# A gated cross-attention and mixture-of-experts layer on one core: the routing arithmetic in fewer and smaller pieces, the last block's down products behind the first small tile, one gather sooner

## The chip, the cores and the metric

The kernel runs on one core of a Trainium2 chip. The metric is device time of one execution in microseconds (us), lower is better. The profile names the engines PE (TensorE, matrix products; PEld is its weight load), DVE (VectorE), ACT (ScalarE), POOL (GpSimd) and SP (SyncE, which only issues transfers here).

## The reference

The input is 4 x 1024 rows of 256 numbers. First each row attends, after a layer norm, to 77 context rows with 16 heads, and the output projection times tanh(g) is added to the row. Then comes the feed-forward part, which is all that the change touches:

```python
scores = softmax(xf @ gate_w.T)             # 4 experts
topk_w, topk_idx = top_k(scores, 2); topk_w /= topk_w.sum() + 1e-20
g = silu(xf @ eg[e].T); u = xf @ eu[e].T    # each expert, 256 -> 688
y = sum over e of comb[:, e] * ((g * u) @ ed[e].T)
y = y + (silu(xf @ sg.T) * (xf @ su.T)) @ sd.T   # the shared expert
x = x + tanh(g_ffn) * y
```

xf is the layer norm of the attended rows, 4096 of them, each sent to 2 of 4 experts, so there are 8192 row copies.

## The kernel before

**Stages.** The rows are worked in 16 units of 256. From 0 to about 308 us attention for all units runs, with the shared expert of units 0 to 6 woven in. From about 308 to 460 us ("late units" 7 to 15) the shared expert goes on, and between its pieces lie two other things: the transposes that bring the routed experts' matrices into place (`e_T(G)` on PE, then `e_hi(G)` on ACT and `e_lo(G)` on DVE, which split each into a high and a low part), and the routing arithmetic. From 460 to 773 us come 13 big blocks of 512 row copies that share one expert, from 773 us on 15 small tiles of 128 copies.

**Order.** Every engine has its own list of steps, written out by hand, and runs it in that order; a step waits on semaphores for what it needs. So a step that is late holds back all behind it on its engine. A unit n of the shared expert is, on PE, `gate_up(n, c)` for six chunks c = 0 to 5 and `down(n)`; on ACT `gate(n, c)` and `h_hi(n, c)`; on DVE `inner(n, c)` (two instructions, lines 2040 and 2045), `last_lo(n)` (line 2049) and `result(n)` (line 2058); on POOL `xn_lo(n)` and `h_lo(n, c)`. The waits that matter below:

- `gate_up(n, 3)` waits for `inner(n, 0)`, `gate_up(n, 4)` for `inner(n, 1)`, `gate_up(n, 5)` for `result(n - 1)`, which frees its bank.
- `down(n)` waits for `last_lo(n)`, and that for `h_hi(n, 5)`, and that for `inner(n, 5)`.
- `e_T(G)` waits for `e_lo(G - 2)`, since two banks are used in turn.
- ACT's list has `gate(9, 3)` behind `e_hi(5)`, which needs `e_T(5)`.

**Routing on DVE.** Its parts are small instructions on 4 to 128 numbers per partition, each linked to the next by a semaphore (`link`): `ranks()` (running counts per expert), `weights()`, `counts()` (reads what `bases()` on PE left in p_t: how many copies each expert gets), `starts()` (where each expert's blocks and small tiles begin), `numbered()`, `position(0)`, `position(1)`, `tiles_and_rows()`; `experts_of_tiles()` says which expert a block or tile has. `places(g)` and `rows_at(g)` (lines 2425, 2429) then build, for g = 0 to 7, 0/1 matrices whose product `spread(g)` on PE (line 3076) makes the table `slot_id` of rows, for the gathers.

**From big blocks to small tiles.** A block j has chunks c = 0 to 5: `big_gate_up` (line 619), `big_inner` and `big_h_lo` on DVE, `big_down(j, c)` (line 636) for t = 0 to 3, each t being 128 rows; t = 0, 1 go to bank p_f[0] and t = 2, 3 to p_f[1]. Chunks 4 and 5 of the last block's down products (24 and 8 products) are done before the small tiles begin. `big_result` (line 582, four times) moves p_f to big_yout, and POOL adds big_yout to the output rows by indirect DMA (line 505, four of them). A small tile j is, on PE, `gate_up(j)` (line 339, 18 calls in the profile's records), `x_T(j + 1)` (line 324, transposes of the gathered rows), `down(j - 1)` (line 350, 354), `hidden_T(j)` (line 364). Its DVE steps are the product `hid` (lines 294, 297), `x_lo(j + 1)` (line 274), `result(j - 1)` (line 286), and the low parts (lines 306 to 310). POOL gathers rows by an indirect DMA (line 199) and adds by another (line 220). Gathers 0 and 1 are issued one block before the end, gather 2 only after the last block's four adds. `hidden_T` writes its transposes to the two banks p_f, so `hidden_T(0)` first waits until the last `big_result` has read them.

Of the kernel before, what the change touches and what calls it, by code (L numbers as in the profile page):

```python
# [8 lines left out]
ALU = mybir.AluOpType  # L9
# [3 lines left out]
P = 128  # L13
# [134 lines left out]
def small_tiles(nc, v, sem, place, banks, s_add):  # L148
# [55 lines left out]
    def on_gpsimd(pool):  # L204
        gather = gathers(pool)

        def add(j, k):
            if not (isinstance(j, int) and j == 0):
                pool.wait_ge(s_add, added + 16 * (j - 1))
            pool.tensor_copy(add_at[k][:, :], slot_id[:, bass.ds(j + AFTER, 1)]).then_inc(s_add_at, 1)  # L210
            pool.wait_ge(s_add_at, j + 1)
            if isinstance(j, int) and j >= SM - 2:
                pool.wait_ge(s_add, added + 16 * j)
                settle(pool)
                pool.wait_ge(s_yo, j + 1)
            else:
                pool.wait_ge(s_yo, j + 1)
                pool.wait_ge(s_add, added + 16 * j)
                settle(pool)
            pool.indirect_dma_start(out, bass.IndirectOffsetOnAxis(add_at[k][:, :], 0),  # L220
                                    yout[k][:, :], None, compute_op=ALU.add).then_inc(s_add, 16)

        gather(2, 0)
        for j in range(2):
            gather(j + 3, 1 - j)
            add(j, j)
        with pool.Fori(1, (SM - 3) // 2) as h:
# [50 lines left out]

    def on_vector(dve):
        x_lo = x_low(dve)  # L280
# [8 lines left out]
        def step(j, k):  # L289
# [8 lines left out]
                                    p_gu[:, FF + CUT:2 * FF].unsqueeze(1).broadcast_to(twice),  # L298
                                    sil[:, CUT:FF].unsqueeze(1).broadcast_to(twice), ALU.mult).then_inc(s_dup, 1)
            if not last:  # L300
                x_lo(j + 1)
# [27 lines left out]
    def on_tensor(pe):  # L329
# [27 lines left out]

        def hidden_T(j):
            pe.wait_ge(s_hid, j + 1)
            wait(pe, s_hlo, j)  # L360
            for c in range(FC):
                if c == FC - 1:
                    pe.wait_ge(s_dup, j + 1)
                last = nc.tensor.transpose(p_h[c // 4][:, (c % 4) * P:(c % 4 + 1) * P], hid[:, c * P:(c + 1) * P],
                                           ident[:, :])
            last.then_inc(s_hT, 1)
# [39 lines left out]

        def run(gate_banks, hidden_banks):
            gate_banks()

            def step(j, k):  # L410
                fixed = isinstance(j, int)
                gate_up(j, expert(k))
                if not (fixed and j == SM - 1):
                    x_T(j + 1, 1 - k)
                if not (fixed and j == 0):
                    down(j - 1, expert(1 - k))
                if not (fixed and j == SM - 1):
                    hold(j + 1, 1 - k)
                if fixed and j == SM - 1:
                    last_hidden_T(j)  # L420
                else:
                    if fixed and j == 0:
                        hidden_banks()
                    hidden_T(j)
            hold(0, 0)
            tiles(pe, step)
            last_down(SM - 1, expert((SM - 1) % 2))
# [7 lines left out]
def big_tiles(nc, v, m, place, banks):  # L435
# [153 lines left out]
    def on_tensor(pe):  # L589
# [32 lines left out]

        def down(j, c):
            n = FC * j + c
# [7 lines left out]
            r = height(c) if c < FC - 1 else P  # L632
            for t in range(BT):
                at = slice(t * P, (t + 1) * P)
# [13 lines left out]
def attend_share_route(nc, v):  # L648
# [8 lines left out]
    with st:  # L657
# [37 lines left out]
        for k in range(2):  # L695
# [82 lines left out]
        w_parts = [sb(f"w_{s}", [P, NE], f32r) for s in ("hi", "lo")]  # L778
        tile_at, te, hit = (sb(n, [1, NX]) for n in ("tile_at", "te", "hit"))
        spare = sb("spare", [P, NS])  # L780
# [38 lines left out]
                                        "spare": rest.sb},  # L819
                           (p_s[:, 0:GUB, :].rearrange("p b n -> p (b n)"), p_m, p_f, p_t), s_add)  # L820
        big = big_tiles(nc, v, {"s_rows": s_rows, "s_xT": s_xnT, "s_xhi": s_xnhi, "s_xlo": s_xnlo, "s_whi": s_whi,
# [252 lines left out]
        def _(pool):  # L1074
# [360 lines left out]
            for j in range(NB):  # L1435
                if j + 2 < NB:
                    big_gather(j + 2)
                if j == NB - 2:
                    small_gather = late["gathers"](pool)
                    small_gather(0, 0)  # L1440
                    small_gather(1, 1)
                big_adds(j)
            late["gpsimd"](pool)
# [498 lines left out]
        def _(dve):  # L1942
# [411 lines left out]
            def counts():  # L2354
                dve.wait_ge(s_base, 1)
                link(nc.vector.tensor_copy(base[:, :], p_t[:, 0:E]))
                link(nc.vector.tensor_copy(count[:, :], p_t[:, E:2 * E]))
# [4 lines left out]
            def starts():  # L2362

                for e in range(1, E):
                    link(tt(blocks[:, e:e + 1], blocks[:, e - 1:e], blocks[:, e:e + 1], ALU.add))
                link(ts(big_end[:, :], blocks[:, :], float(NB), float(WIDE), ALU.min, ALU.mult))
                link(tt(rest_n[:, :], count[:, :], big_end[:, :], ALU.subtract))
                link(tt(rest_n[:, 1:E], rest_n[:, 1:E], big_end[:, 0:E - 1], ALU.add))
                link(ts(rest_n[:, :], rest_n[:, :], float(P - 1), None, ALU.add))
                link(nc.vector.tensor_copy(whole_i[:, :], rest_n[:, :]))  # L2370
# [4 lines left out]
                dve.wait_ge(s_zero, 10)  # L2375
                for e in range(1, E):
                    link(tt(small_at[:, e:e + 1], small_at[:, e - 1:e], rest_n[:, e - 1:e], ALU.add))
                link(nc.vector.scalar_tensor_tensor(out=jump[:, :], in0=small_at[:, :], scalar=float(AFTER * P),
                                                    in1=big_end[:, :], op0=ALU.add, op1=ALU.subtract))
                link(ts(base[:, :], base[:, :], -1.0, None, ALU.add))  # L2380
                link(tt(base[:, 1:E], base[:, 1:E], big_end[:, 0:E - 1], ALU.add))

            def numbered():
                wide_e = [P, E, NT]
                link(tt(cum[:, :, :], cum[:, :, :], base[:, :].unsqueeze(2).broadcast_to(wide_e), ALU.add))
                over = ttmp[:, :, :].rearrange("p t e -> p (t e)").rearrange("p (e t) -> p e t", e=E)
# [15 lines left out]
            def experts_of_tiles():  # L2402
                dve.wait_ge(s_iota, 7)
                link(nc.vector.tensor_copy(tile_at[:, :], tile_at_i[:, :]))
                for e in range(1, E):
                    into = te if e == 1 else hit
                    link(ts(into[:, 0:NB], tile_at[:, 0:NB], big_end[0:1, e - 1:e], None, ALU.is_ge))
                    link(ts(into[:, NB:NX], tile_at[:, NB:NX], small_at[0:1, e:e + 1], None, ALU.is_ge))
                    if e > 1:
                        link(tt(te[:, :], te[:, :], hit[:, :], ALU.add))  # L2410
                link(nc.vector.tensor_copy(expert_of[:, :], te[:, :]))
# [29 lines left out]
            def late_units():  # L2441
# [24 lines left out]
                e_lo(2)  # L2466
                inner(8, 3)
                inner(8, 4)
                e_lo(3)
                inner(8, 5)  # L2470
                e_lo(4)

                last_lo(8)
                weights()
                inner(9, 0)
                counts()
                starts()
                inner(9, 1)
                numbered()
                position(0)  # L2480
                position(1)
                tiles_and_rows()
                result(8)
                inner(9, 2)
                inner(9, 3)
                e_lo(5)
                inner(9, 4)
                inner(9, 5)
                e_lo(6)
# [20 lines left out]
                e_lo(11)  # L2510
                rows_at(2)
                inner(11, 0)
                e_lo(12)
# [42 lines left out]
                e_lo(21)  # L2556
                experts_of_tiles()
                places(7)
# [71 lines left out]
            for j in range(NB):  # L2630
                for c in range(FC):
                    big_step(j, c)
            for t in range(BT):
                big_result(NB - 1, t)
            late["vector"](dve)

        @block.tensor
        def _(pe):
# [442 lines left out]
            def late_units():  # L3081
# [154 lines left out]
            for j in range(NB):  # L3236
                for c in range(FC):
                    big_step(j, c)
            big_down(NB - 1, FC - 2)
            big_down(NB - 1, FC - 1)  # L3240
            late["tensor"](pe)(lambda: pe.wait_ge(s_hid, FC * (NU + NB)), lambda: pe.wait_ge(s_y, NU + 2 * NB))

# [24 lines left out]
```

## Time and profile before

| | us |
|---|---|
| median of 3 runs (890.25 to 891.5) | 890.29 |
| the profiled execution | 891.95 |
| its span, first to last instruction | 890.2 |
| PE busy | 851.2 (96% of the span) |
| DVE busy | 599.7 (67%) |
| ACT busy | 521.2 (59%) |
| POOL busy | 459.9 (52%) |

The mean granted TensorE clock is 0.986 of full speed (2.4 GHz). A row of the timeline gives start, duration, engine, line, operation and operands; in brackets is how long the engine sat idle before it and what ended that. "x3" is three instructions merged. PE's records are pipelined, so its pace is read from the distance of starts, not from durations.

### The profile page before, as it was taken

What the parts mean: (1) busy time and instruction counts of PE and PEld (TensorE: products, weight loads), DVE (VectorE), ACT (ScalarE), POOL (GpSimd) and SP (SyncE); (2) the same over time, 40 slices, a digit from 0 to 9 for tenths busy, and PEclk for the clock granted to TensorE, in tenths of its full rate; (3) what the DMA queues carried; (4) which work ended last, traced back from release to release, by engine and by line L of the source; (5) the groups of instructions that cost most, each with busy time, mean ns of one, the idle gap of its engine ahead of it and who ended that gap; (6) DMA issues with size and microseconds to landing.
All of it is one profiled execution on the core that took longest, in us unless ns stands there. A gap on an engine that the chain in (4) does not pass through costs nothing.

```text
span 890.2 us, 19216 instructions
## 1 busy us (share of the span) xinstructions
PE 851.2 (96%) x6271; PEld 745.9 (84%) x6272; DVE 599.7 (67%) x1259; ACT 521.2 (59%) x1846; POOL 459.9 (52%) x551
## 2 busy tenths in 40 slices
PE   8888999999999898999999999999999999989995
PEld 6566788878888798999988888888888888889994
DVE  6899899999998578878775555555555555434442
ACT  4989999999999343656464544444444544222221
POOL 5686767667665442676431454444444443444442
PEclk9799999999999999999999999999999999999998
DMA  7125223222312222423240333222222222232221
GB/s 217 41 79 175 68 89 93 89 66 91 101 62 85 71 73 68 135 84 119 82 142 24 49 48 48 46 39 41 38 42 42 43 46 36 31 45 45 35 37 22
DMA packets 56889, 62.06 MB, mean 70 GB/s; under 512 B 15643, under 2 KB 45184, under 8 KB 56800
## 3 DMA queue, kind: packets, MB, share of 16 engines
q1 hardware_dynamic: 42871, 43.15, 15.5%
q0 software_dynamic: 12864, 17.57, 12.5%
q8 instruction: 48, 0.79, 0.4%
q10 hardware_dynamic: 1064, 0.21, 0.1%
q14 instruction: 42, 0.34, 0.1%
HBM read 34.78 MB, written 25.82 MB: 68 GB/s over the span
## 4 chain that ended last, share of the span: by engine, by line
PE 82%; DVE 7%; ACT 4%; issue 3%; DMA 2%; POOL 1%; SPq 0%; DVEq 0%; POOLq 0%; ACTq 0%
PE p_s L619 22%; PE p_f L636 12%; PE p_f L2755 8%; PE p_s L339 6%; PE p_f L2800 4%; PE p_s L2755 4%; PE p_t L2686 3%; ACT prob L1478 3%; PE p_s L2672 3%; PE p_t L350 3%; PE p_m L2713 3%; PE p_m L2701 2%; PE p_m L2653 2%; PE p_s L2800 1%; PE p_s L2858 1%
## 5 line engine op out<-in xcount | busy, mean ns | idle before, releaser
L505 POOL DMA_INDIRECT out_rows<-big_yout,slot_id x52 | 86.5, 1664 | 156.4 <-DVE big_yout L582 144.6
L1478 ACT ACTIVATE prob<-p_s,negmax 128x77 f32<-128x77 f32 x512 | 161.2, 372 | 8.2 <-DVE negmax L2023 8.0
L533 ACT ACTIVATE big_sil<-p_s 128x512 f32<-128x512 f32 (+1 forms) x78 | 46.6, 597 | 143.3 <-PE p_s L619 143.3
L1478 ACT ACTIVATION_READ_ACCUMULATOR prob<-p_s,negmax 128x1 f32 x512 | 129.1, 255 | 0.0
L565 DVE TENSOR_TENSOR big_hid<-p_s,big_sil 128x512 f32<-128x512 f32 (+1 forms) x78 | 54.0, 692 | 99.5 <-ACT big_sil L533 99.5
L619 PE MATMUL p_s<-big_fxT_hi,big_w_hi 128*128 128x512 f32 (+1 forms) x286 | 113.9, 398 | 0.2 <-DVE big_w_lo L558 0.2
L619 PE MATMUL p_s<-big_fxT_lo,big_w_hi 128*128 128x512 f32 (+1 forms) x286 | 112.8, 394 | 0.0
L619 PE MATMUL p_s<-big_fxT_hi,big_w_lo 128*128 128x512 f32 (+1 forms) x286 | 112.2, 392 | 0.0
L1104 POOL TENSOR_TENSOR prob<-prob,rinv 128x616 f32<-128x616 f32 x64 | 78.5, 1236 | 62.3 <-DVE rinv L2030 62.3
L1123 POOL TENSOR_TENSOR shT_lo<-shid,shT_hi 128x256 fp32r<-128x256 f32 x80 | 63.2, 801 | 49.3 <-ACT shT_hi L1517 49.0
L636 PE MATMUL p_f<-wd_hi,big_hT_hi 128*128 (+1 forms) x312 | 85.6, 280 | 0.1
L636 PE MATMUL p_f<-wd_lo,big_hT_hi 128*128 (+1 forms) x312 | 85.3, 279 | 0.0
L2755 PE MATMUL p_f<-xnT_hi,swgu_hi 128*128 128x256 f32 x248 | 75.7, 305 | 2.0 <-DVE shid L2045 2.0
L636 PE MATMUL p_f<-wd_hi,big_hT_lo 128*128 x260 | 72.7, 280 | 0.0
L2755 PE MATMUL p_f<-xnT_hi,swgu_lo 128*128 128x256 f32 x248 | 69.7, 281 | 0.0
L2755 PE MATMUL p_f<-xnT_lo,swgu_hi 128*128 128x256 f32 x248 | 69.6, 281 | 0.0
L572 DVE TENSOR_TENSOR big_hT_lo<-big_hid,big_hT_hi 128x512 fp32r<-128x512 f32 (+1 forms) x65 | 44.9, 690 | 35.6 <-ACT big_hT_hi L538 35.6
L497 POOL DMA_INDIRECT big_xin<-xn_scratch,slot_id x52 | 51.3, 987 | 32.1 <-issue 17.2
L619 PEld LDWEIGHTS p_s<-big_fxT_hi,big_w_lo 128*128 128x128 f32 (+1 forms) x286 | 53.1, 186 | 13.0
L538 ACT ACTIVATE big_hT_hi<-big_hid 128x512 fp32r<-128x512 f32 (+1 forms) x78 | 49.3, 632 | 23.1 <-DVE big_hid L565 23.1
L636 PEld LDWEIGHTS p_f<-wd_hi,big_hT_hi 128*128 128x128 f32 (+1 forms) x312 | 58.7, 188 | 3.7 <-issue 0.3
L619 PEld LDWEIGHTS p_s<-big_fxT_hi,big_w_hi 128*128 128x128 f32 (+1 forms) x286 | 53.1, 186 | 10.2 <-issue 0.3
(336 smaller groups left out, 2561.3 us busy)
## 6 DMA issues: line engine op xcount, KB each, us to landing
xr<-in_x SPq DMA_DIRECT2D x16, 256.0 KB, 2.9
x_scratch<-xr SPq DMA_DIRECT2D x16, 256.0 KB, 2.5
xn_scratch<-xn SPq DMA_DIRECT2D x16, 256.0 KB, 2.1
xt_scratch<-xnT SPq DMA_DIRECT2D x16, 256.0 KB, 2.6
xin<-xt_scratch SPq DMA_DIRECT2D x16, 256.0 KB, 3.6
x1in<-x_scratch SPq DMA_DIRECT2D x16, 256.0 KB, 3.3
out_rows<-syout SPq DMA_DIRECT2D x16, 256.0 KB, 2.4
raw<-in_L_ffn_ed SPq DMA_DIRECT2D x4, 688.0 KB, 4.4
```

The lines of the kernel that those rows point to most:

```text
L339: last = nc.tensor.matmul(p_gu[:, g0:g1], fxT[a][:, c, :], wgu[b][:, bass.ds(e * KC + c, 1), g0:g1], start=(c == 0 and q == 0), stop=(c == ...
L497: pool.indirect_dma_start(xin[:, t, :], None, v["xn_d"], bass.IndirectOffsetOnAxis(slot_id[:, column(j, t)], 0)).then_inc(s_rows, 16)
L505: pool.indirect_dma_start(out, bass.IndirectOffsetOnAxis(slot_id[:, column(j, t)], 0), yout[:, t, :], None, compute_op=ALU.add).then_inc(s ...
L533: act.activation(sil[n % 2][0:r, :], p_gu[c % 2][0][0:r, :], ACT.Silu).then_inc(s_sil, 1)
L538: act.activation(hT[n % 3][0][0:r, :], hid[n % 2][0:r, :], ACT.Copy).then_inc(s_hhi, 1)
L565: nc.vector.tensor_tensor(hid[n % 2][0:r, :], up, sil[n % 2][0:r, :], ALU.mult).then_inc(s_hid, 1)
L619: last = nc.tensor.matmul(p_gu[c % 2][half][0:out_rows, :], lhsT, fxT[j % 2][x][:, k, :], start=(k == 0 and q == 0), stop=(k == KC - 1 and ...
L636: last = nc.tensor.matmul(p_y[t // 2][:, t % 2 * H:(t % 2 + 1) * H], hT[n % 3][h][0:r, at], wd[w][0:r, bass.ds(e * FC + c, 1), :], start=( ...
L1104: pool.tensor_tensor(pr_, pr_, rinv[:, t, m * HH:(m + 1) * HH].unsqueeze(2).broadcast_to([P, HH, SK]), ALU.mult).then_inc(s_P, 1)
L1123: pool.tensor_tensor(hT[1][:, c, :], hid[:, c, :], hT[0][:, c, :], ALU.subtract).then_inc(s_hlo, 1)
L1478: last = act.activation(prob[n % 2][t][:, m * PW + h * SK:m * PW + (h + 1) * SK], p_s[:, 2 * t + h // 4, col:col + SK], ACT.Exp, bias=negm ...
L2755: last = nc.tensor.matmul(bank[:, j * UT * P:(j + 1) * UT * P], swgu[w][:, k, j * SGU + c * P:j * SGU + (c + 1) * P], xns[x][:, n % 2, k, ...
```

## The change

The change has four parts.

1. *Routing on DVE, and `bases()` on PE.* In `counts()` the copy of `base` is taken out (it moves to the end of `starts()`); in `starts()` two chains of three additions become one scan each, a tensor_scalar is folded into its neighbour, and another into `numbered()`. In `experts_of_tiles()` compare and add become one instruction.
2. *Other places.* `bases()` moves from behind `gate_up(8, 5)` to behind `gate_up(8, 3)`. `weights()` goes from unit 9 to before `inner(8, 4)`, `counts()` to before `inner(8, 5)`, `starts()` before `inner(9, 0)`; `numbered()` and `result(8)` follow `inner(9, 1)`; `position(0)`, `position(1)` and `tiles_and_rows()` come behind `inner(9, 2)`, `inner(9, 3)` and `inner(9, 4)`. `experts_of_tiles()` goes from unit 14 to unit 11, before `inner(11, 0)`.
3. *Last block.* `big_down(12, 4)` is split: t = 0, 1 stay before `gate_up(0)` of the small tiles; t = 2, 3 and all of chunk 5 come behind it. The four `big_result(12, t)` move behind the product `hid` of small tile 0 on DVE. The small tiles' transposes use the banks p_s[3] and p_f[0], and only chunk 4 of `hidden_T(0)` waits, for the first two results.
4. *Gather 2* is issued before the last block's four adds on POOL, not after them.

```diff
@@ gathers and banks
-        gather(2, 0)
         for j in range(2):
             gather(j + 3, 1 - j)
             add(j, j)
...
+                if j == NB - 1:
+                    small_gather(2, 0)
                 big_adds(j)
...
-                           (p_s[:, 0:GUB, :].rearrange("p b n -> p (b n)"), p_m, p_f, p_t), s_add)
+                           (p_s[:, 0:GUB, :].rearrange("p b n -> p (b n)"), p_m, (p_s[:, 3, :], p_f[0]), p_t), s_add)
@@ small tiles, on DVE and PE
+            if isinstance(j, int) and j == 0:
+                last_results()
             if not last:
                 x_lo(j + 1)
...
             for c in range(FC):
+                if c == 4 and second_bank:
+                    second_bank()
...
                 gate_up(j, expert(k))
+                if fixed and j == 0:
+                    last_of_blocks()
@@ routing arithmetic
-                link(nc.vector.tensor_copy(base[:, :], p_t[:, 0:E]))
...
-                for e in range(1, E):
-                    link(tt(blocks[:, e:e + 1], blocks[:, e - 1:e], blocks[:, e:e + 1], ALU.add))
-                link(ts(big_end[:, :], blocks[:, :], float(NB), float(WIDE), ALU.min, ALU.mult))
-                link(tt(rest_n[:, :], count[:, :], big_end[:, :], ALU.subtract))
+                link(nc.vector.tensor_tensor_scan(big_end[:, :], fresh[0][:, 0:E], blocks[:, :], 0.0, ALU.mult, ALU.add))
+                link(ts(big_end[:, :], big_end[:, :], float(NB), float(WIDE), ALU.min, ALU.mult))
+                link(nc.vector.scalar_tensor_tensor(out=rest_n[:, :], in0=count[:, :], scalar=float(P - 1),
+                                                    in1=big_end[:, :], op0=ALU.add, op1=ALU.subtract))
                 link(tt(rest_n[:, 1:E], rest_n[:, 1:E], big_end[:, 0:E - 1], ALU.add))
-                link(ts(rest_n[:, :], rest_n[:, :], float(P - 1), None, ALU.add))
...
-                for e in range(1, E):
-                    link(tt(small_at[:, e:e + 1], small_at[:, e - 1:e], rest_n[:, e - 1:e], ALU.add))
+                link(nc.vector.tensor_tensor_scan(small_at[:, 1:E], fresh[0][:, 0:E - 1], rest_n[:, 0:E - 1], 0.0,
+                                                  ALU.mult, ALU.add))
...
-                link(ts(base[:, :], base[:, :], -1.0, None, ALU.add))
+                link(nc.vector.tensor_copy(base[:, :], p_t[:, 0:E]))
...
-                link(tt(cum[:, :, :], cum[:, :, :], base[:, :].unsqueeze(2).broadcast_to(wide_e), ALU.add))
+                link(nc.vector.scalar_tensor_tensor(out=cum[:, :, :], in0=cum[:, :, :], scalar=-1.0,
+                                                    in1=base[:, :].unsqueeze(2).broadcast_to(wide_e),
+                                                    op0=ALU.add, op1=ALU.add))
@@ experts_of_tiles
-                for e in range(1, E):
-                    into = te if e == 1 else hit
-                    link(ts(into[:, 0:NB], tile_at[:, 0:NB], big_end[0:1, e - 1:e], None, ALU.is_ge))
-                    link(ts(into[:, NB:NX], tile_at[:, NB:NX], small_at[0:1, e:e + 1], None, ALU.is_ge))
-                    if e > 1:
-                        link(tt(te[:, :], te[:, :], hit[:, :], ALU.add))
+                for a, b, ends in ((0, NB, big_end[0:1, 0:E - 1]), (NB, NX, small_at[0:1, 1:E])):
+                    link(ts(te[:, a:b], tile_at[:, a:b], ends[:, 0:1], None, ALU.is_ge))
+                    for e in range(1, E - 1):
+                        link(nc.vector.scalar_tensor_tensor(out=te[:, a:b], in0=tile_at[:, a:b], scalar=ends[:, e:e + 1],
+                                                            in1=te[:, a:b], op0=ALU.is_ge, op1=ALU.add))
@@ DVE's list, units 8, 9, 11 and 14
                 inner(8, 3)
+                weights()
                 inner(8, 4)
                 e_lo(3)
+                counts()
                 inner(8, 5)
                 e_lo(4)
 
                 last_lo(8)
-                weights()
+                starts()
                 inner(9, 0)
-                counts()
-                starts()
                 inner(9, 1)
                 numbered()
-                position(0)
-                position(1)
-                tiles_and_rows()
                 result(8)
                 inner(9, 2)
+                position(0)
                 inner(9, 3)
+                position(1)
                 e_lo(5)
                 inner(9, 4)
+                tiles_and_rows()
                 inner(9, 5)
...
                 rows_at(2)
+                experts_of_tiles()
                 inner(11, 0)
...
                 e_lo(21)
-                experts_of_tiles()
                 places(7)
@@ PE's list
                 gate_up(8, 3)
+                bases()
                 gate_up(8, 4)
                 e_T(3)
                 gate_up(8, 5)
-                bases()
                 e_T(4)
...
+            def last_of_blocks():
+                big_down(NB - 1, FC - 2, BT // 2, BT)
+                big_down(NB - 1, FC - 1)
...
+            big_down(NB - 1, FC - 2, 0, BT // 2)
+            late["tensor"](pe)(banks_of_gate, last_of_blocks, bank_of_hidden)
```

## Rows read from the trace of the kernel before

**Rows 1.** The page: the span.
```profile
span 890.2 us, 19216 instructions
```

**Rows 2.** Waits of PE: us in total, times, longest.
```profile
PE p_s L2755 <- DVE syout L2058: 2.6, 1, 2.6
PE p_m L324 <- DMA xin<-xn_scratch,get_at: 2.2, 1, 2.2
PE p_f L2755 <- DVE shid L2045: 2.0, 2, 1.2
...
PE p_f L364 <- DVE hid L294: 1.6, 1, 1.6
...
PE p_m L3076 <- DVE at_row L2429: 1.2, 1, 1.2
```

**Rows 3.** PE by stretches: length, busy, instructions, granted clock, DMA.
```profile
353.00:361.00 8.00, 5.42 (x29) 0.79 0.28 98
426.00:431.00 5.00, 3.85 (x32) 1.00 0.34 108
782.00:791.00 9.00, 6.85 (x37) 0.81 0.25 46
```

**Rows 4.** Timeline of DVE, units 8 and 9.
```profile
329.34 0.42 DVE L2305 TENSOR_TENSOR_SCAN seen<-fresh,eq 128x128 f32<-128x128 f32 x1
...
338.90 0.42 DVE L2040 SCALAR_TENSOR_TENSOR th<-th,p_s 128x256 f32<-128x256 f32 x1
...
341.87 0.65 DVE L2049 TENSOR_TENSOR shT_hi<-shid,shT_hi 48x256 fp32r<-48x256 f32 x1
342.55 0.54 DVE L2347 SCALAR_TENSOR_TENSOR weight<-top,tgf,den 128x32 f32<-128x32 f32 x2
...
343.74 0.42 DVE L2040 SCALAR_TENSOR_TENSOR th<-th,p_f 128x256 f32<-128x256 f32 x1 [0.17 <-DVE w_lo L2351]
...
345.53 0.55 DVE L2365 TENSOR_TENSOR blocks<-blocks 128x1 f32<-128x1 f32 x3
346.11 1.29 DVE L2366 TENSOR_SCALAR big_end<-blocks 128x4 f32<-128x4 f32 x1
...
350.43 0.42 DVE L2040 SCALAR_TENSOR_TENSOR th<-th,p_f 128x256 f32<-128x256 f32 x1
```

**Rows 5.** Timeline of POOL in the same stretch.
```profile
346.08 1.29 POOL L1117 TENSOR_TENSOR xnT_lo<-xin,xnT_hi 128x512 fp32r<-128x512 f32 x1 [3.85 <-ACT xnT_hi L1502]
```

**Rows 6.** Timeline of PE: first product of `down(8)`; there is no idle time before it.
```profile
343.14 0.29 PE L2800 MATMUL p_s<-swd_hi,shT_hi 128*128 128x256 f32 x1
```

**Rows 7.** The chain that ended last, by start and length, units 9 to 14.
```profile
362.84 1.76 PE p_f L2800 x15
...
421.15 0.28 DVE tile_at L2404
...
424.47 0.18 DVE expert_of L2411
```

**Rows 8.** The same chain, last block and small tiles.
```profile
769.55 2.81 PE p_f L636 x24
...
797.34 3.76 PE p_s L339 x18
...
804.02 3.77 PE p_s L339 x18
```

**Rows 9.** Timelines of DVE, POOL and PE behind the last block.
```profile
773.23 1.66 DVE L582 TENSOR_SCALAR big_yout<-p_f,slots 128x256 f32<-128x256 f32 x4 [0.94 <-PE p_f L636]
774.93 1.55 POOL L505 DMA_INDIRECT out_rows<-big_yout,slot_id  x1 [9.90 <-DVE big_yout L582]
780.51 1.55 POOL L505 DMA_INDIRECT out_rows<-big_yout,slot_id  x1 [0.30 <-issue]
783.10 1.04 POOL L199 DMA_INDIRECT xin<-xn_scratch,get_at  x1 [0.83 <-POOL get_at L196]
785.95 0.44 PE L324 MATMUL p_m<-ident,xin 128*128 128x128 f32 x2 [2.15 <-DMA xin<-xn_scratch,get_at]
```

More of the change, by code:

```diff
@@ L277, in x_low, with on_vector @@
         return x_lo
-    def on_vector(dve):
+    def on_vector(dve, last_results):
         x_lo = x_low(dve)
@@ L356, in down, with hidden_T @@
             last.then_inc(s_y, 1)
-        def hidden_T(j):
+        def hidden_T(j, second_bank=None):
             pe.wait_ge(s_hid, j + 1)
@@ L405, in expert, with run @@
             return pe.snap(held[k], min_val=0, max_val=E - 1)
-        def run(gate_banks, hidden_banks):
-            gate_banks()
+        def run(banks_of_gate, last_of_blocks, bank_of_hidden):
+            banks_of_gate()
             def step(j, k):
@@ L421, in step @@
                 else:
-                    if fixed and j == 0:
-                        hidden_banks()
-                    hidden_T(j)
+                    hidden_T(j, bank_of_hidden if fixed and j == 0 else None)
             hold(0, 0)
@@ L621, in gate_up, with down @@
             last.then_inc(s_gu, 1)
-        def down(j, c):
+        def down(j, c, t0=0, t1=BT):
             n = FC * j + c
@@ L632, in down @@
             r = height(c) if c < FC - 1 else P
-            for t in range(BT):
+            for t in range(t0, t1):
                 at = slice(t * P, (t + 1) * P)
@@ L778, in attend_share_route @@
         w_parts = [sb(f"w_{s}", [P, NE], f32r) for s in ("hi", "lo")]
-        tile_at, te, hit = (sb(n, [1, NX]) for n in ("tile_at", "te", "hit"))
+        tile_at, te = (sb(n, [1, NX]) for n in ("tile_at", "te"))
         spare = sb("spare", [P, NS])
@@ L2632, in _, with last_results @@
                     big_step(j, c)
-            for t in range(BT):
-                big_result(NB - 1, t)
-            late["vector"](dve)
+            def last_results():
+                for t in range(BT):
+                    big_result(NB - 1, t)
+            late["vector"](dve, last_results)
         @block.tensor
@@ L3238, in _, with banks_of_gate, bank_of_hidden @@
                     big_step(j, c)
-            big_down(NB - 1, FC - 2)
-            big_down(NB - 1, FC - 1)
-            late["tensor"](pe)(lambda: pe.wait_ge(s_hid, FC * (NU + NB)), lambda: pe.wait_ge(s_y, NU + 2 * NB))
+            def banks_of_gate():
+                pe.wait_ge(s_hid, FC * (NU + NB))
+            def last_of_blocks():
+                big_down(NB - 1, FC - 2, BT // 2, BT)
+                big_down(NB - 1, FC - 1)
+            def bank_of_hidden():
+                pe.wait_ge(s_y, NU + 2 * NB - 1)
+            big_down(NB - 1, FC - 2, 0, BT // 2)
+            late["tensor"](pe)(banks_of_gate, last_of_blocks, bank_of_hidden)
 _INS = ['x', 'ctx_1024', 'mask_Bx1xSxS2_if1', 'g_xattn', 'g_ffn', 'L0_xattn_w_q', 'L0_xattn_b_q', 'L0_xattn_w_k',
```

## The prediction

> **What bounds the kernel now.** I read the page first: the span is 890.2 us [rows 1] and PE is busy for 96% of it, so a change can only win where PE waits or runs slowly. The second view is the list of PE's waits [rows 2]. Five of them lie where the change works: 2.6 us for `result(8)` (before `gate_up(9, 5)`), 1.2 us for `inner(9, 1)` (the longest of the two that make up 2.0 us), 1.2 us for `rows_at(7)`, 1.6 us for the product `hid` of small tile 0, and 2.2 us for gather 2. That is 8.8 us. The third view, PE by stretches with the granted clock [rows 3], adds what no list of waits shows: from 353 to 361 us the mean granted clock is 0.79, from 782 to 791 us it is 0.81. Both stretches hold a wait of over 2 us, and in each the clock went to the lower of its two levels behind it: 8 x 0.21 = 1.7 us and 9 x 0.19 = 1.7 us of PE time. From 426 to 431 us PE also waited 1.2 us, and the clock stayed at 1.00. Last, DVE's timeline [rows 4] and the chain [rows 7] show why units 8 and 9 wait: the chain leaves PE and goes through DVE's small pieces.
>
> **Units 8 to 10: DVE's order.** Before, `weights()` takes from 342.55 to 343.74, `inner(9, 0)` 0.8 from there, `counts()` with five pieces the 1.0 up to 345.53, about 0.2 each, and `starts()` goes from 345.53 to 350.43 [rows 4]. `starts()` has 17 pieces; three additions take 0.55, so 17 x 0.2 = 3.4 us, and the rest are two pieces that last far longer than their like: big_end takes 1.29 [rows 4], exactly while POOL's xnT_lo takes 1.29 [rows 5]. Now `starts()` has 12 pieces, or 2.4 us, `counts()` 0.8. The scans of 4 and 3 numbers are not in the trace: below 0.18 (one of the three additions) they can't be much, and one of 128 numbers takes 0.42 [rows 4]; I take 0.2, nearest by size; the upper end adds 0.4 in all.
>
> Now `weights()` and `counts()` come ahead of `inner(8, 5)`, and with it of `h_hi(8, 5)`, `last_lo(8)` and `down(8)`. DVE from 338.90 [rows 4]: `weights()` 1.2, `inner(8, 4)` 0.9, `e_lo(3)` 0.3, `counts()` 0.8, `inner(8, 5)` 0.9, `e_lo(4)` 0.65, `last_lo(8)` 0.45, together 5.2, so 344.1; before, `last_lo(8)` was over at 342.5, and PE came to `down(8)` at 343.14 without idling [rows 6]. With 0.25 for one piece that meets POOL, `down(8)` starts at 344.35: **a new wait of 1.2 us** (1.0 to 2.0). `bases()` itself only changes places on PE (0.5 us either way), and `ranks()` is done 1 us before it.
>
> Then `starts()`, `inner(9, 0)`, `inner(9, 1)` end 2.4 + 1.8 = 4.2 us after 344.3, just as `down(8)` (4.0 us) ends; `gate_up(9, 3)` and `(9, 4)` need them 1.4 and 2.8 us later. The wait of 1.2 is gone. `numbered()` (1.3, with a stall 2.3) and `result(8)` (0.7) are done 3 us later, well before `gate_up(9, 5)` at 5.0 us or more behind `down(8)`: the wait of 2.6 is gone too, and with it the low clock.
>
> What is late next is `e_lo(6)`, for which `e_T(8)` waits. PE's own work from `down(8)` to the first product of `down(9)` is 362.84 - 343.14 [rows 6, 7] less waits of 3.8 and 1.7 of clock, 14.2 us, 13.4 up to `e_T(8)` once the starts after waits are off. DVE: `gate(9, 3)` can't come before `e_T(5)` and `e_hi(5)`: 4.0 for `down(8)`, 4.3 for three chunks, 0.3, 0.4 and 0.4 for these three make 9.4 us after `down(8)` starts; from there `inner(9, 3)` 0.9, `position(1)` 0.75, `e_lo(5)` 0.25, `inner(9, 4)` 0.9, `tiles_and_rows()` 1.15, `inner(9, 5)` 0.9, `e_lo(6)` 0.6 make 14.8, so PE waits 1.4 us. Two of the pieces can meet POOL's `h_lo`, up to 0.6 each; I take one, 2.0. Sum: 3.8 + 1.7 of before against 1.2 + 2.0, **2.3 us gained**, 3.4 without any stall and 0.3 if the clock falls again.
>
> The row with big_end shows a DVE piece held until POOL's was over. The Trainium skill (SBUF — State Buffer, "Who interferes with whom") states the rule: copy, cast and tensor_scalar forms in a 2-port mode, and forms with two SBUF inputs against a GpSimd instruction that reads SBUF, share a port pair with GpSimd, and the later one is blocked in full. By it the new places, beside four `h_lo`, are as exposed as the old one beside `xn_lo(10)`, and all four chances on the path taken, 2.4 us, would leave 0.8 us; by the plain durations it would be 3.2.
>
> **Units 11 and 14.** `experts_of_tiles()` lasts from 421.15 to 424.65 [rows 7], one piece of it 1.3 long, and stands in the chain ahead of `rows_at(7)`. Gone from there, DVE is 3.5 us earlier, so `spread(7)`'s wait of 1.2 [rows 2] goes, with 0.2 for the slow start behind it: **1.4 us**. In unit 11 it costs 8 pieces, 2.0 us, 3.1 if it meets `xn_lo(12)`. `gate_up(11, 3)` needs `inner(11, 0)` some 3.5 us after DVE had it; DVE idles 5 us later in that unit. I take 0.1, at most 0.8. Moving the gains through units 10 to 15 costs nothing: DVE, ACT and transfers are released by PE's own steps there, and PE has no other wait.
>
> **The last block and small tiles.** The block's chunk 4 began at 769.4 (its second product opens the chain's entry at 769.55), 24 products in 2.8 us [rows 8]. Now 12 of them end at 770.8; `gate_up(0)` waits only for the last `big_inner` (770.9) and lasts 3.76 [rows 8], to 774.7; then 12 + 8 products, 2.35, and `x_T(1)` 0.2, to 777.3. The product `hid` is done on DVE by then (it took 1.8 from the end of `gate_up`), so the wait of 1.6 goes. But `last_results()` (1.66 [rows 9]) can start only at 776.8, when chunk 5's t = 1 is in the bank, and `x_lo(1)` (0.4) is queued behind it: 778.9. PE, through with `hidden_T(0)` at 777.95, waits 0.95 for it. From `gate_up(1)` at 778.95 two periods of 804.02 - 797.34 = 6.7 [rows 8] lead to `gate_up(3)` at 792.3; it was 797.34. Gather 2, now issued at about 767, is long there. Gather 3 is next: POOL's four adds start 0.9 behind the second result (777.6), at 778.5, the fourth 5.6 later as before (774.93 to 780.51), gather 3 another 2.6 later (to 783.10) [rows 9], at 786.7, and the rows are there 2.85 later, as for gather 2 (783.10 to 785.95): 789.55, against 789.4 when PE asks. So 0.2 is lost, and `gate_up(3)` starts at 792.5. With 0.1 for a slower start, **4.7 us gained** (3.0 to 5.0); 1.7 of it is the low clock, which needs both old waits to be gone. The adds that follow are 2 us ahead of PE's need.
>
> **Sum.** 2.3 + 1.4 - 0.1 + 4.7 = 8.3 us. The span of 890.2 becomes 881.9, the profiled execution's 891.95 becomes 883.65. The median of the runs shown, 890.29, is 1.7 below that execution, and becomes **882.0 us**. On this kernel 0.2% (1.8 us) is about what a measurement can tell from no change.
>
> **Rivals.** (a) *The clock falls at the new wait before `e_T(8)`.* For it: my wait is 2.0, and 2.6 and 2.2 made it fall; against: 1.2 did not. It costs 1.7: 883.7.
> (b) *The tail gives half.* `x_lo(1)` behind four results and a gather 3 that is late by 1 us make two waits close together; if the clock falls there as before, 1.7 + 0.8 are lost: 884.5.
> (c) *More than the sum.* No piece meets POOL, and `e_lo(6)` is in time: 880.6.
> (d) *Slower.* Twenty small pieces now stand before `last_lo(8)` and `inner(9, 0)`. If each were held as big_end was (1.29 for 0.2), PE would stand 22 us: 904. It decides from 0.5 us a piece (8.3 + 1.8 over 20). Against it: POOL idled 3.85 us before its piece at 346.08 [rows 5].
> (e) *No change.* The late units end by something PE doesn't set, such as the last expert's matrices, and the tail by the chain of adds: 889 to 891. Against it: PE's few waits.
>
> The Trainium skill (TensorE: Matmul & The Clock Gate, "HAM oscillation") says that waits inside a loop throttle the clock again and again. The trace agrees at two places, 0.79 and 0.81. By it rival (a), 883.7, is as likely as my sum; the 1.2 us wait that left the clock at 1.00 is why I put it lower.
>
> **Chances.** The sum 0.48; (a) 0.24; (b) 0.12; (c) 0.10; (d) 0.03; (e) 0.03. The sum's own range is 881.2 to 883.0. For 8 in 10 I go from 880.4 to 884.9, which takes in (a), (b) and most of (c). All but (d) and (e) are faster by over 1.8 us: 0.94; same 0.03; slower 0.03.
>
> **What the next profile would show.** PE's waits: `syout` (2.6), `hid` (1.6), gather (2.2) and `at_row` (1.2) gone; new ones before line 2800 (for `shT_hi`, 1.2), before line 2858 (for `wgu_lo`, 2.0) and before line 339 (for fxT_lo, 0.95), and one below 0.5 for gather 3. The granted clock at 1.00 behind the small tiles' start. `down(9)` at about 360.5, line 619's start at 455.6, `gate_up(3)` 8.4 earlier than 797.34. I am wrong if `down(8)` waits over 2 us, if the clock is low in either stretch, or if the four results hold `x_lo(1)` for more than 1 us.

## The result, and the profile after

The changed kernel takes **885.80 us** (median of 5 runs, 884.64 to 886.48), the kernel before 890.42 (5 runs). The ratio is 0.9944, 95% interval 0.9930 to 0.9959: faster by 0.56%, where I had forecast 0.93% (882.0) and a range up to 884.9. The sign was right; the gain is 4.6 us instead of 8.3.

The span and PE's waits of the changed kernel, with us in total, times and the longest, to be set beside [rows 1, 2]:

```profile
span 884.8 us, 19214 instructions
```

```profile
PE p_s L2862 <- DVE wgu_lo L2084: 1.8, 1, 1.8
...
PE p_s L2807 <- issue: 1.3, 2, 1.1
...
PE p_s L340 <- DVE fxT_lo L273: 0.8, 1, 0.8
...
PE p_m L3083 <- POOL at_val L1331: 0.7, 1, 0.7
...
PE p_f L367 <- DVE big_yout L585: 0.3, 1, 0.3
```

The waits for `syout` (2.6), `inner(9, 1)` (1.2), `hid` (1.6) and gather 2 (2.2) are gone. In their place stand the new ones that I had named: 1.1 before `down(8)` (line 2807; forecast 1.2), for which the profile names no engine ("issue"), 1.8 before `e_T(8)` (2.0), 0.8 before `gate_up(1)` (0.95). Two I had not: 0.7 before `spread(7)`, now for POOL, and 0.3 for the results of the block's second half. PE by stretches, columns as in [rows 3]:

```profile
356.00:360.00 4.00, 2.17 (x18) 1.92 (x17) 3.70 (x11) 1.89 (x6) 0.80 (x2) 1.00 0.52 176
360.00:362.00 2.00, 2.00 (x13) 2.00 (x12) 1.93 (x6) 0.20 (x1) 1.28 (x1) 0.57 0.00 0
362.00:364.00 2.00, 2.00 (x12) 2.00 (x12) 2.00 (x3) 1.52 (x7) 1.47 (x1) 0.58 0.00 0
364.00:366.00 2.00, 2.00 (x20) 2.00 (x19) 1.34 (x2) 0.70 (x4) 2.00 (x2) 1.00 0.04 8
782.00:791.00 9.00, 9.00 (x63) 8.14 (x62) 4.38 (x10) 2.91 (x6) 6.11 (x8) 1.00 0.51 68
```

Behind the small tiles' start the clock is at 1.00 (before 0.81). But behind the new wait before `e_T(8)` it falls: from 360 to 364 us it is 0.57 and 0.58. PE is busy without a gap there and starts 25 products in these 4 us, and 20 in the next 2; 2 x 0.43 + 2 x 0.42 = 1.7 us are lost. That is rival (a), in the very profile by which I had said it would show. The chain around it:

```profile
358.73 0.70 DVE wgu_lo L2084
359.43 0.04 issue
359.48 0.66 PE p_s L2862 x4
360.13 3.12 PE p_f L2807 x15
363.26 0.43 PE p_f L2810 x2
363.68 1.82 PE p_f L2807 x15
```

The same 15 products take 3.12 us at the lower level and 1.82 at the full clock ([rows 7]: 1.76). `down(9)` starts at 359.97; it was 362.6, and 0.44 of the difference was there ahead of the first edited place, so 2.2 us are gained up to it, against the 2.3 of my sum. Then 1.55 go again.

Unit 14, timelines of ACT, POOL and PE:

```profile
424.96 0.42 ACT L1522 ACTIVATE shT_hi<-shid 128x256 fp32r<-128x256 f32 x1 [1.90 <-PE p_f L2810]
```
```profile
425.46 0.74 POOL L1126 TENSOR_TENSOR shT_lo<-shid,shT_hi 128x256 fp32r<-128x256 f32 x1 [2.13 <-ACT shT_hi L1522]
426.15 2.08 POOL L1331 TENSOR_TENSOR at_val<-at_til,w_lo 128x544 fp32r<-128x544 f32 x1
```
```profile
428.38 0.33 PE L3083 MATMUL p_m<-at_val,at_row 128*128 128x204 f32 x1 [0.72 <-POOL at_val L1331]
```

DVE is out of the way, and `spread(7)` now waits for POOL's `low_shares(7)`. It is queued behind `h_lo(14, 0)`, that waits for ACT's `h_hi(14, 0)`, and that for `down(13)`; POOL and ACT idle about 2 us ahead of it. Of the 1.4 us that I had put down here the trace shows 0.45.

The tail, DVE's timeline and the chain:

```profile
774.97 0.82 DVE L293 TENSOR_TENSOR hid<-p_s,sil 128x640 f32<-128x640 f32 x1 [4.05 <-ACT sil L254]
775.71 0.28 DVE L296 TENSOR_TENSOR hid<-p_s,sil 128x128 f32<-128x128 f32 x1
775.91 1.65 DVE L585 TENSOR_SCALAR big_yout<-p_f,slots 128x256 f32<-128x256 f32 x4
777.48 0.41 DVE L273 TENSOR_TENSOR fxT_lo<-p_m,fxT_hi 128x256 fp32r<-128x256 f32 x1
```
```profile
768.18 2.10 PE p_f L639 x18
770.29 3.88 PE p_s L340 x18
...
778.05 4.02 PE p_s L340 x18
...
784.99 3.77 PE p_s L340 x18
788.75 0.34 PE p_m L325 x2
...
791.91 3.76 PE p_s L340 x18
```

`gate_up(0)` starts 2.1 us behind the 768.02 at which the last 18 products begin, not 1.5: the 24 products of [rows 8] are 12 of chunk 3 and 12 of chunk 4 (chunk 4 has 12, not the 24 of the description above), so 18 stay ahead of `gate_up(0)`, not 12. Six fewer follow it, 14 and not 20, so PE is through with them when I said (`hidden_T(0)` begins 7.85 us behind 768.02, forecast 7.9); what is late is `hid`, and with it the four results. `gate_up(1)` waits 0.78 for `x_lo(1)`, which stands behind the four results as forecast. The third tile's rows are 0.15 late for `x_T(3)` (forecast 0.2). `gate_up(3)` comes at 791.66.

### The profile page after: what moved, and what is told of

Its sections match the earlier page's. It is cut to its first block, busy times and chain, and to the rows that moved or that the text cites. A ratio compares the mean times of both kernels' runs of the same rounds, so it can differ in the third digit from the quotient of the medians.

```text
span 884.8 us, 19214 instructions
## 1 busy us (share of the span) xinstructions
PE 850.1 (96%) x6271; PEld 744.7 (84%) x6272; DVE 596.7 (67%) x1251; ACT 520.7 (59%) x1846; POOL 460.8 (52%) x551
## 4 chain that ended last, share of the span: by engine, by line
PE 84%; DVE 5%; ACT 5%; issue 3%; DMA 1%; POOL 1%; SPq 0%; DVEq 0%; POOLq 0%; ACTq 0%
PE p_s L622 22%; PE p_f L639 12%; PE p_f L2762 8%; PE p_s L340 6%; PE p_f L2807 5%; PE p_s L2762 4%; ACT prob L1483 3%; PE p_t L2693 3%; PE p_s L2679 3%; PE p_t L351 3%; PE p_m L2708 2%; PE p_m L2660 2%; PE p_m L2720 2%; PE p_s L2807 2%; PE p_s L2865 1%
```

## The experiments

All times are medians; each run's ratio is to runs of the kernel before on the same chip, whose medians were 890.52, 889.93, 890.26 and 890.66. So two versions are compared by their ratios (0.001 is 0.9 us), and a variant whose interval overlaps the changed kernel's, 0.9930 to 0.9959, isn't told from it by its time. Two intervals compare the traces, since they don't depend on the first 300 us, in which the executions differ by up to 3 us: **U**, from the first product of `logits(14)` (300.43 in the kernel before) to that of the first block's first `gate_up` (459.24), which the expectation of `e_best` calls `logits(15)` and the second `gate_up`; **T**, from the first product after the last block's last `gate_up` to `gate_up(3)` of the small tiles. Each is given with whether the clock fell in it.

**The two halves apart.** `a_routing` has the edits in units 8 to 14, `a_tail` those of the last block and of gather 2, both on the kernel before.

> The kernel before with the edits of units 8 to 14 alone (scans, order of DVE's pieces, experts_of_tiles in unit 11, bases() one chunk later); the last block and the small tiles as before. Theory 1 (this part brought only what the start of the unit stage's end moved, 1.36 less the 0.44 that was there ahead of the change's first place): 0.9 us gained, 889.4. Theory 2 (my prediction's size, with the loss elsewhere): 3.6 us, 886.7. Theory 3 (the clock in this part is a matter of chance from run to run): between 889.4 and 887.8, with the single times spread over more than 1 us.

> The kernel before with the edits of the last block and of the small gather alone. Theory 1 (the parts add up): 4.1 us gained, 886.3. Theory 2 (the tail brings the 4.7 predicted): 885.7. Rival (part of the tail's gain comes from the earlier units' state): below 3.5 us, above 886.9.

`a_routing`: 888.95, ratio 0.9982 (0.9973 to 0.9991). `a_tail`: 887.50, ratio 0.9969 (0.9959 to 0.9978). 1.6 and 3.0 together are the 4.6 of the whole, so the parts add up, and the tail's is 1.1 below what the two first profiles had shown. That is the number of `a_tail`'s rival, but not its reason: T is 23.7 as in the changed kernel, with nothing changed in the earlier units. What is missing is the clock, since the low stretch in the tail isn't in every execution of the kernel before, as shown below. The single times of `a_routing` go from 887.4 to 890.6, as theory 3 said.

**Gather 2 alone, and the split alone.**

```diff
-        gather(2, 0)                      # start of the small tiles' part of POOL
+                if j == NB - 1:           # a_gather: ahead of the last block's adds
+                    small_gather(2, 0)
```

`a_split` has the rest of the tail's edits, with gather 2 left where it was.

> The kernel before with gather 2 of the small tiles issued ahead of the last block's adds, nothing else. Theory 1 (the low clock needs a wait of over 2 us, and the wait of 1.6 for hid alone leaves it high): the 2.2 of wait and the 1.7 of clock both go, 3.5 to 3.9 us gained, 886.5. Theory 2 (the wait of 1.6 is enough to lower the clock): only 2.2 gained, 888.1. Rival (the adds are held by the gather ahead of them and gather 3 is late in its place): under 1 us.

> The kernel before with the last block's down products split around gate_up(0) and the four results behind hid, gather 2 still behind the four adds. Theory 1 (gather 2's landing sets the tail, and the adds ahead of it now start 4.0 later, 778.9 instead of 774.93): 4 us slower, 894.3. Rival 1 (the adds are not what holds gather 2): within 0.5 of 890.4. Rival 2 (PE's own work sets the tail once the wait for hid is gone): 1.6 faster, 888.8.

`a_gather`: 888.29, ratio 0.9978 (0.9968 to 0.9987); T is 23.8, against 26.1 to 27.7 before and 23.7 with both edits. The median is that of theory 2, but the trace isn't: the clock is at 1.00 all through the tail. `a_split`: 896.79, ratio 1.0066 (1.0054 to 1.0078). PE's waits there:

```profile
PE p_m L326 <- DMA xin<-xn_scratch,get_at: 6.6, 1, 6.6
PE p_s L341 <- DVE fxT_lo L274: 0.8, 1, 0.8
PE p_f L368 <- DVE big_yout L586: 0.3, 1, 0.3
```

Gather 2's rows come 20.7 us behind the start of T, before it was 16.6: the 4 us by which the adds ahead of it start later. The clock is low from 789.6 to 796.4, the first 1.8 us of it within the wait, and PE takes 5.14 us from `x_T(2)` to `gate_up(2)`, 2.84 in the changed kernel: 2.3 lost. By the adds alone (theory 1) 4 us would have been lost. So gather 2's place is worth 2.3 of the tail's 2.5 us at the full clock, and the split 0.1: it takes away 1.57 of wait and puts 0.33 and 0.78 in its place; of the 0.37 by which `gate_up(1)` is then earlier, 0.27 are gone by `gate_up(3)`, since gather 3 is late. Alone the split is a loss of 6 us.

**The wait before `e_T(8)`.** `b_rows_early` moves two steps into DVE's idle 1.9 us; `b_fill` gives PE work that nobody reads.

```diff
                 position(0)
+                position(1)
+                tiles_and_rows()
                 inner(9, 3)
-                position(1)
                 e_lo(5)
                 inner(9, 4)
-                tiles_and_rows()
```
```diff
+                keep_warm(14)             # b_fill: 14 transposes of the identity
                 e_T(8)
                 down(9)
```

> The changed kernel with position(1) and tiles_and_rows() moved up ahead of inner(9, 3), into the 1.92 us in which DVE waits there for ACT. Theory 1 (e_lo(6) is all that e_T(8) waits for, and the wait is what can lower the clock behind it): in the profile no wait before e_T(8), down(9) starts 1.8 earlier against down(8) (14.1 instead of 15.9 behind it) and the granted clock is 1.00 from 353 to 370; 3.5 us less than the changed kernel's profile in units 9 and 10, and 2.5 to 3.5 in the median, 882.3 to 883.3. Rival (something else is just as late, such as ACT's e_hi or the transfer of the matrix): under 1 us, above 884.8.

> The changed kernel with 14 transposes of the identity in front of e_T(8), some 1.7 us of work that nobody reads, in the place where PE waits 1.83 us. Theory 1 (it is PE's idling there that lowers the clock): e_T(8) starts when it did, the wait before it is under 0.2, the clock stays at 1.00 from 356 to 370, and units 9 and 10 take 1.7 less; median up to 1.7 lower, 884.1 to 885. Rival (the clock falls for another reason, such as the slower work before it): it falls as before and the time stays at 885.8.

`b_rows_early`: 884.42, ratio 0.9940 (0.9927 to 0.9953). No wait before `e_T(8)`, `down(9)` 13.8 behind `down(8)` (it was 15.9), the clock at 1.00, `gate_up(10, 2)` 3.7 us nearer to `down(8)`. The span is 881.4 against 884.8, but the median only 1.4 lower, and by the ratios 0.4: outside what I expected. `b_fill`: 885.84, ratio 0.9951 (0.9938 to 0.9964). `e_T(8)` starts when it did, the clock stays at 1.00, and the stage is 1.6 shorter in the profile; the median doesn't move. Both results fit a fall at this place in a part of the executions only; they don't show it, since the intervals overlap.

**Does it fall each time?** The kernel before, three more profiles.

> The kernel before, unchanged, profiled again. Theory 1 (the clock's fall behind a wait is a matter of chance): the waits are the same to 0.2 us, and at least one of the two stretches (behind the waits of 1.2 and 2.6, behind gather 2's of 2.2) stays at 1.00 in at least one of these three profiles. Theory 2 (my prediction's: a wait of over 2 us lowers it): it is low in both stretches in all three.

> The kernel before, unchanged, the second of three profiles; theories 1 and 2 as for the first: by theory 1 one of the two stretches stays at 1.00 in one of the three or more, by theory 2 both are low in all three.

> The kernel before, unchanged, the third of three profiles; theories 1 and 2 as for the first: by theory 1 one of the two stretches stays at 1.00 in one of the three or more, by theory 2 both are low in all three.

The stretches behind the two waits, in the first and in the second of them:

```profile
356.00:362.00 6.00, 4.06 (x31) 3.77 (x32) 5.65 (x16) 2.70 (x10) 2.21 (x3) 1.00 0.41 133
...
786.00:792.00 6.00, 6.00 (x33) 5.76 (x33) 1.50 (x3) 1.26 (x3) 1.23 (x3) 0.72 0.09 23
```
```profile
356.00:362.00 6.00, 5.76 (x32) 5.28 (x33) 4.94 (x14) 3.19 (x9) 2.21 (x4) 0.72 0.43 140
...
786.00:792.00 6.00, 6.00 (x41) 5.50 (x40) 2.09 (x5) 1.26 (x3) 1.91 (x3) 1.00 0.16 28
```

Same program, same waits (2.6 and 2.1 in both), and the clock falls behind the one or the other; in the third it falls in unit 9 alone. Over all traces that have the same wait:

```
wait                                 clock fell   in
unit 9: 1.2, then 2.6                  5 of 7     3 of before's 4, a_tail, a_split; not in a_gather
small tiles: 1.6, then 2.1             2 of 5     2 of before's 4; not in a_routing
before e_T(8): 1.8                     3 of 7     after, a_routing, b_experts; not in b_weights,
                                                  c_unit14, c_xlo, c_xlo_gather3

            U, clock fell   U, full clock   T, clock fell   T, full clock
before          158.7           157.3           27.7            26.1
changed         157.9           156.4            -              23.65
```

(U and T with the part's edits, from all traces that have them.) Theory 2, mine, is refuted.

**`weights()` later, `experts_of_tiles()` back.**

```diff
-                weights()                 # b_weights: from ahead of inner(8, 4)
...
                 position(0)
+                weights()
```
```diff
-                experts_of_tiles()        # b_experts: from ahead of inner(11, 0)
...
                 e_lo(21)
+                experts_of_tiles()
                 places(7)
```

> The changed kernel with weights() (1.19 us on DVE) taken out from ahead of inner(8, 4) and put behind position(0), into DVE's idle 1.92 us. Theory 1 (DVE's order sets down(8)): the wait of 1.11 before down(8) goes and everything behind it is 1.1 earlier, the wait before e_T(8) staying near 1.8: 884.7. Rival 1 (what is gained at down(8) is lost again at e_T(8), since DVE's work up to e_lo(6) is the same): the wait before e_T(8) grows to 2.9 and the time is the same.

> The changed kernel with experts_of_tiles() back in front of places(7) in unit 14, nothing else. Theory 1 (in unit 14 POOL's low_shares(7) was next behind rows_at(7), so the move brought 0.45 and cost 0.2 in unit 11): 0.2 to 0.4 us slower in the profile between units 11 and 14, the wait before spread(7) 1.1 for at_row, and nothing that the median can tell. Theory 2 (my prediction): 1.3 us slower, 887.1.

`b_weights`: 886.01, ratio 0.9949 (0.9937 to 0.9962). The wait of 1.11 before `down(8)` goes, 0.64 comes before `e_T(7)`, 1.84 stays before `e_T(8)`: of 1.1 us some 0.5 reach `down(9)` (U 155.9 against 156.4), between the theory's 1.1 and the rival's nothing. `b_experts`: 886.70, ratio 0.9959 (0.9946 to 0.9972). The time is as near to theory 2 (887.1) as to no change and can't decide; the trace does. The wait before `spread(7)` is 0.75, for `at_row`, and U is 0.2 *shorter* than in the changed kernel's profile. The move of `experts_of_tiles()` brought nothing; I had put it down for 1.3.

**What was next: unit 14 and the tail.**

```diff
-                h_lo(14, 0)               # c_unit14, POOL
                 low_shares(7)
+                h_lo(14, 0)
...
-                h_hi(14, 0)               # c_unit14, ACT
                 shares_at(7)
+                h_hi(14, 0)
```
```diff
-                last_results()
+                last_results(0, BT // 2)
                 x_lo(j + 1)
+                last_results(BT // 2, BT)
```

> The changed kernel with POOL's low_shares(7) ahead of h_lo(14, 0) and ACT's shares_at(7) ahead of h_hi(14, 0), both in idle time of their engines. Theory 1 (POOL's and ACT's order is what was next behind the wait that went in unit 14): in the profile the wait of 0.72 before spread(7) goes, and gate_up(14, 3) starts 0.7 to 0.9 earlier against the start of down(13); median 885.0. Rival (DVE's at_row, in rows_at(7) behind result(13), is as late): the wait is then for at_row and shrinks by less than 0.3.

> The changed kernel with results 2 and 3 of the last block behind x_lo(1) on DVE instead of ahead of it. Theory 1 (the four results hold x_lo(1), and gather 3 is next): the wait of 0.78 before gate_up(1) goes, so gate_up(2) is 0.8 earlier, but gather 3 comes in when it did, so gate_up(3) is only 0.1 to 0.2 earlier. Rival (gather 3 isn't what sets gate_up(3)): gate_up(3) is 0.8 earlier too, median 885.0.

> As c_xlo, and gather 3 of the small tiles issued ahead of the last block's adds too, just behind gather 2. Theory 1 (gather 3 is the next limit and POOL has time for it there): no wait for gathers, gate_up(3) 0.9 to 1.0 earlier than in the changed kernel, median 884.8. Rival (the adds, now behind a gather that waits for x_T(1), start about 1 us later and one of the next gathers or results is late for it): 0.2 or less.

`c_unit14`: 885.33, ratio 0.9946 (0.9927 to 0.9966). No wait before `spread(7)`; U is 155.3 against 156.4, both at the full clock. `c_xlo`: 886.47, ratio 0.9955 (0.9940 to 0.9971). The 0.78 goes, and gather 3 takes it:

```profile
PE p_m L327 <- DMA xin<-xn_scratch,get_at: 0.6, 1, 0.6
PE p_f L369 <- DVE big_yout L587: 0.3, 1, 0.3
```

T is 23.6, 0.1 shorter. With gather 3 ahead of the adds too: 884.98, ratio 0.9945 (0.9930 to 0.9961), T 22.6, 1.0 shorter; 0.2 of it is given back by `gate_up(4)`.

**All together, and the best of it.** `d_all` joins all of this, with `weights()` ahead of `places(0)` and `experts_of_tiles()` ahead of `inner(11, 5)`; `e_best` leaves these two where the change had them.

> The changed kernel with everything together: position(1) and tiles_and_rows() in DVE's idle time of unit 9, weights() only ahead of places(0), experts_of_tiles() in DVE's idle time at the end of unit 11, low_shares(7) and shares_at(7) in POOL's and ACT's idle time of unit 14, results 2 and 3 behind x_lo(1), gather 3 ahead of the last adds. Theory 1 (each removes its own wait, nothing is next): 1.1 (down(8)) + 1.8 (e_T(8)) + 0.2 (unit 11) + 0.8 (unit 14) + 0.9 (tail) = 4.8 us of the profile's stages, and the clock's 1.7 wherever it fell: median 879.5 to 881. Rival (as with the change itself, the next work in line gives part of it back): 882 to 884.

> The changed kernel with position(1) and tiles_and_rows() in DVE's idle time of unit 9, low_shares(7) and shares_at(7) in POOL's and ACT's idle time of unit 14, results 2 and 3 behind x_lo(1), and gather 3 ahead of the last adds; weights() and experts_of_tiles() where the change put them. Theory 1 (the gains of the single steps add up: 1.95 in units 9 and 10, 1.06 in unit 14, 1.0 in the tail, and the clock's 1.7 in the share of executions where it fell behind e_T(8)'s wait): units 8 to 15 take 153.3 us from logits(15) to the first block's second gate_up, against 156.3 of the changed kernel at the full clock, and the median is 881 to 882.5. Rival (what the all-together version lost came from the moved shares, not from weights() and experts_of_tiles()): 155.5 us there, 883.5 to 884.5.

`d_all`: 883.98, ratio 0.9928 (0.9914 to 0.9941). U is 155.5, only 0.9 less, with new waits of 0.9 before `e_T(7)`, 0.4 for `h_lo` in unit 10 and 0.2. `e_best`: **882.86**, ratio 0.9919 (0.9901 to 0.9937), 2.9 below the changed kernel's median and 2.2 by the two ratios, whose intervals overlap. U is 155.1, and not the 153.3 that I expected; in `b_rows_early` it was 154.1 without unit 14's gain. DVE and POOL in `e_best` show what came between:

```profile
345.15 0.16 DVE L2387 COPY base<-p_t 128x4 f32<-128x4 f32 x1
345.34 1.25 DVE L2388 TENSOR_TENSOR base<-base,big_end 128x3 f32<-128x3 f32 x1
```
```profile
345.28 1.29 POOL L1123 TENSOR_TENSOR xnT_lo<-xin,xnT_hi 128x512 fp32r<-128x512 f32 x1 [4.20 <-ACT xnT_hi L1511]
```

The last piece of `starts()` meets POOL's `xn_lo(10)` and lasts 1.25 instead of 0.16; in `b_rows_early` `xn_lo(10)` started at 346.47, after `starts()`. `e_T(7)` waits 1.36. In `c_unit14` the same piece is held too, 1.18 us beside a POOL piece that began 0.12 earlier, and PE has no new wait there; in `b_rows_early` the order is that of `e_best` and the piece isn't held, and there is none either. So by these traces, one each, it takes both, the held piece and `position(1)` and `tiles_and_rows()` ahead of `inner(9, 3)`. Whether they meet hangs on some 0.1 us (in the changed kernel the piece was over 0.03 before POOL's began).

The tail gives back too. T is 22.6 in `e_best`, 1.0 shorter, but from `gate_up(3)` to the end of the span the traces take 93.1 us in the changed kernel, 93.4 in `c_xlo_gather3`, 93.7 in `d_all` and 93.9 in `e_best`, where `x_T(4)` waits 0.32 for gather 4, which POOL issues only behind the adds. So of the 1.0 some 0.2 is left there.

## Why the prediction was right or wrong

**Units 8 to 10: the steps held.** `starts()` 2.33 us for 12 pieces (forecast 2.4), the scans 0.17 each (0.2), `down(8)` waits 1.1 (1.2), `e_T(8)` 1.8 (2.0). By U and the trace of unit 14, at the full clock this part is worth 0.7 us, and my 3.8 of waits less 3.2 is 0.6. The bounds that I set beside the 2.3 don't follow from its terms, though: without a stall they give 3.2, not 3.4, and with a fall of the clock 0.6, not 0.3.

**The clock: the step that failed.** The sum took 1.7 in unit 9 and 1.7 in the tail as lost before and saved after, "which needs both old waits to be gone", because the profile shown had both and my argument was the length of the wait. Such a fall costs 1.7 us where it comes ([rows 3] and the rows above), of which 1.4 to 1.5 reach the end of U or T, and between 350 and 800 us PE had idled ahead of each. But it comes in 5 of 7, 2 of 5 and 3 of 7 profiled executions with the same waits; so few traces give rough shares. Counted so, before loses 0.71 x 1.4 + 0.4 x 1.5 = 1.6 us and after 0.43 x 1.5 = 0.6: about 1.0 is gained and not 3.4. The profiled execution of before was one with both falls, 1.5 above the median, and I moved its whole gain to the median. Its mean granted clock says how rare that is: 0.986, where the 57 later runs of before lie from 0.988 to 0.993. Rival (a) was in the right place, but neither it nor its absence was the one outcome.

**Unit 14: wrong, 0.45 for 1.4.** I went from DVE's 3.5 us straight to "`spread(7)`'s wait goes" and didn't ask who else `spread(7)` waits for. `c_unit14` shows it: POOL's and ACT's order, worth 1.1. `b_experts` shows that in the changed order the move itself brings nothing. Unit 11's 0.1 was 0.2.

**The tail: mechanism right, 0.5 too large.** At the full clock 2.5 us were gained, I had 4.7 - 1.7 = 3.0. The 0.5 is the miscount of products in [rows 8]: `gate_up(0)` is 0.6 later, with it `hid` and the results, and `gate_up(1)` comes 10.0 us behind the first of the last products, not 9.55. The new wait for `x_lo(1)`, its reason and gather 3's lateness were as forecast. What I did not see is how the gain is split: `a_gather` has nearly all of it.

**Sum.** At the full clock 0.96 (U) + 2.5 (T) = 3.4 us, and 1.0 of clock, 4.4 of the 4.6 measured. My sum had 4.9 and 3.4. Of the 3.9 too much, 2.4 are the clock, 0.95 unit 14, 0.5 the tail. Another way to the same: time multiplied by its mean granted clock, run by run, averages 881.0 over 26 runs of before and 877.5 over the 5 of after, 3.5 apart (other runs of before: 880.8 to 881.6). What the low clock takes is then 9.45 us before and 8.15 after, 1.3 apart, where the shares above gave 1.0.

**Small pieces beside POOL.** Rival (d) needed 0.5 us a piece. Three of the some 20 were held in the changed kernel (`blocks` 0.69, `til_f` 0.72, and `tile_at` 1.27 in unit 11), each ending with a POOL piece. The Trainium skill's rule (SBUF — State Buffer, "Who interferes with whom") says that the later one is blocked in full; the rows of `e_best` agree, 1.25 us beside a POOL piece of 1.29 that began 0.06 earlier. It costs something only where the chain runs through the piece (`e_best`, not `c_unit14`), so a version can lose 1 us to it by a shift of 0.1.

## What to carry to other kernels

When a wait goes, list every engine that the waiting instruction needs, with what each stands behind in its queue; the next of them sets the gain, here 0.45 instead of 1.4. One profile is one draw: a low clock behind a wait counts at the share of executions that have it, so profile the kernel before more than once and compare stages, not spans. A transfer that is issued sooner can be the whole gain of a restructuring (2.3 of 2.5 us), and the same restructuring without it a loss.

## What the runs showed of the hardware

The granted clock fell to its lower level (0.5, that is 1.2 GHz instead of 2.4) in some executions and not in others behind the same wait, 10 times in 19, and each of these falls cost the same 1.7 us. Behind the wait of 6.6 us (`a_split`) it was low for longer, 6.8 us, and cost 2.3. Behind the 1.0 to 1.2 us before `spread(7)` it fell in none of the seven traces that have this wait. The Trainium skill (TensorE: Matmul & The Clock Gate, "HAM oscillation") describes a loop in which the wait for data lowered the clock again in every step; these traces agree that the falls come behind idle stretches, and show that such a stretch doesn't always bring one. Where the wait was taken away (`b_rows_early`) or filled (`b_fill`, 0.30 left) it stayed high, but that is two traces, and with a fall in 3 of 7 two without one come by chance 1 time in 3. What in an execution decides it stays open: the four of the kernel before reach `down(8)` at 342.88, 343.14, 344.53 and 344.59 us, and only the last kept its clock in unit 9, so the moment alone doesn't tell.
